# Decoder layer on one core: prologue products and norms, and the order of the attention loop's last output product and first cross scores

## The reference: what is computed

```python
x = x + self_attn(layernorm(x))          # 16 query heads of 32, 4 key/value heads, rope, softmax, @ W_out
x = x + cross_attn(layernorm(x), ctx)    # q = ln(x @ Wq) per head; k = ln(ctx[:345] @ Wk); v = ctx[:345] @ Wv
                                         # plus a second softmax over the last 16 rows ("dca"), added; @ Wo
x = x + moe(layernorm(x))                # shared expert (1408) + top 4 of 60 experts (352), router on x
```

## Time and profile before

| | |
|---|---|
| median of three runs | 1272.35 us |
| profiled execution | 1271.59 us, span 1269.8 us |
| TensorE busy | 1128.7 us (89%) |
| VectorE, ScalarE, GpSimd busy | 512.8, 259.0, 369.1 us |
| one pair of the loop (205.85 to 362.91) | 157.06 us |
| the loop begins, the last pair's last output product ends | 47.9, about 682 us |

### The profile page before, as it was taken

The page is one execution under the profiler, slowest core; times in us unless marked ns, Lnnn a source line. Parts: engine busy times, 40 slices in busy tenths (PEclk is TensorE's granted clock), DMA queues, the critical chain, the costliest instruction groups (busy, mean ns, idle before and its releaser), DMA issues.

```text
span 1269.8 us, 19035 instructions
## 1 busy us (share of the span) xinstructions
PE 1128.7 (89%) x5590; PEld 606.8 (48%) x5590; DVE 512.8 (40%) x1411; ACT 259.0 (20%) x804; POOL 369.1 (29%) x843
## 2 busy tenths in 40 slices
PE   1899888998889988999887999999898898998898
PEld 0354455444554445544454555554444454454454
DVE  7652565426654266542754561121121121211144
ACT  0141232412324133241331300011110111111100
POOL 3274460754607545075200036000000000000073
PEclk9898899988999889998899999999999998998999
DMA  8999001000010000100202478399999999999654
GB/s 312 335 396 366 13 2 43 23 1 12 2 52 14 1 12 2 53 14 1 89 1 70 123 283 293 121 334 391 390 394 387 391 390 385 388 385 380 241 137 116
DMA packets 76583, 233.08 MB, mean 184 GB/s; under 512 B 11362, under 2 KB 13766, under 8 KB 68814
## 3 DMA queue, kind: packets, MB, share of 16 engines
q1 hardware_dynamic: 58830, 197.90, 42.6%
q10 hardware_dynamic: 11520, 20.98, 4.6%
q0 software_dynamic: 6144, 13.13, 3.5%
HBM read 178.75 MB, written 53.22 MB: 183 GB/s over the span
## 4 chain that ended last, share of the span: by engine, by line
PE 72%; DVE 10%; DMA 9%; issue 6%; SPq 2%; ACT 1%; DVEq 1%; ACTq 0%
PE ps L817 15%; PE ps L1095 10%; PE ps L899 9%; DMA arena<-in_w 8%; PE ps L1162 6%; PE ps L1158 5%; PE ps L1256 5%; PE ps L1193 3%; PE ps L1189 3%; PE ps L888 2%; PE ps L956 2%; PE ps L976 2%; DVE arena L1748 1%; PE ps L947 1%; PE ps L1150 1%
## 5 line engine op out<-in xcount | busy, mean ns | idle before, releaser
L817 PE MATMUL ps<-arena 128*100 128x512 f32 (+3 forms) x576 | 223.8, 535 | 12.7 <-DVE arena L1719 5.5
L756 POOL DMA_INDIRECT arena<-ys_d,slot_u x32 | 37.7, 1179 | 425.9 <-issue 423.9
L817 PEld LDWEIGHTS ps<-arena 128*100 128x100 f32 (+1 forms) x576 | 89.1, 176 | 116.2 <-issue 96.1
L1162 PE MATMUL ps<-arena 128*64 128x352 f32 x640 | 111.7, 507 | 30.3 <-issue 16.0
L1095 PE MATMUL ps<-arena 128*128 128x400 f32 x352 | 121.7, 508 | 6.8 <-DMA arena<-xT_d 6.0
L899 PE MATMUL ps<-arena 128*100 128x512 f32 x256 | 120.9, 616 | 0.0
L1962 DVE COPY arena<-ps 128x512 f32<-128x512 f32 x40 | 27.7, 692 | 229.0 <-PE ps L1150 229.0
L1158 PE MATMUL ps<-arena 128*128 128x352 f32 x320 | 98.1, 459 | 0.8 <-issue 0.8
L682 POOL TENSOR_TENSOR arena<-arena 115x512 f32<-115x512 f32 (+1 forms) x29 | 30.1, 1039 | 227.5 <-DVE arena L1675 158.2
L1330 ACT ACTIVATE arena<-ps,arena 100x345 f32<-100x345 f32 x128 | 69.3, 546 | 132.2 <-DVE arena L1748 130.7
L1095 PEld LDWEIGHTS ps<-arena 128*128 128x128 f32 x352 | 67.7, 193 | 59.4 <-issue 8.4
(11 more groups left out here) (218 smaller groups left out, 1521.6 us busy)
## 6 DMA issues: line engine op xcount, KB each, us to landing
arena<-in_w SPq DMA_DIRECT2D x60, 1408.0 KB, 12.2
arena<-in_w SPq DMA_DIRECT2D x60, 512.0 KB, 13.3
xs_d<-zero SPq DMA_DIRECT2D x5, 3328.0 KB, 26.2
arena<-in_w SPq DMA_DIRECT2D x60, 192.0 KB, 13.9
arena<-xs_d ACTq DMA_DIRECT2D x40, 256.0 KB, 7.8
ys_d<-arena ACTq DMA_DIRECT2D x40, 256.0 KB, 7.5
ys_d<-zero SPq DMA_DIRECT2D x2, 3328.0 KB, 24.7
arena<-in_se_up SPq DMA_DIRECT2D x11, 512.0 KB, 6.9
```

The lines of the kernel that those rows point to most:

```text
L817: last = nc.tensor.matmul(ps[0:m, k, 0:cols[1] - cols[0]], lhs(c), w[:, c, cols[0]:cols[1]], start=(c == 0), stop=(c == n_c - 1))
L1162: last = nc.tensor.matmul(ps[half * HALF:(half + 1) * HALF, 3 + gu, 0:I], xsT[1][:, c, half * HALF:(half + 1) * HALF], w13_s[s][1 + half][ ...
```

## The change

- Prologue: the six context products stand ahead of the transposes of the dca keys, in banks (2, 3, 5) and (6, 7, 0). The three key norms are one sequence: three squares into one tile of 3 x 512, one sum over it, one inverse root on 48 columns, three scalings.
- TensorE: the fourth part of the first output product stands ahead of kx(1,2) and vx(1,1), which stand behind the transposes of the second sequence's probabilities. vx(1,2), kx(0,0) and the second xT2 stand inside step 0, with two products of zeros behind them. The query projection of sequence 1 goes from step 0 to step 1, vx(0,0) from step 6 to 5. The zeros of steps 1 and 5 go from (0, 2) and (2, 3) to (0, 0) and (0, 2).
- VectorE: the second layernorm of x is interleaved with the four maxima of step 0.
- GpSimd: both dca_blocks stand ahead of head_norm((1, 2)).

The diff, without the lines of the fill table, the names of tiles and ScalarE's order, which follows TensorE's:

```diff
--- before.py
+++ after.py
...
@@ -109,9 +111,9 @@
 
 
 
-STEP_HOOKS = {0: [("xq", 1)], 1: [("kx", 0, 0)], 2: [("kx", 0, 1)], 3: [("xqT", 1)], 4: [("kx", 0, 2), ("ds", 1)],
-              5: [("dpT", 0), ("rx", 0)], 6: [("vx", 0, 0), ("xo", 0)], 7: [("vx", 0, 1)], 8: [("dpT", 1)]}
-STEP_ZEROS = {1: (0, 2), 2: (0, 2), 3: (2, 3), 4: (0, 2), 5: (2, 3), 6: (0, 2), 7: (0, 2), 8: (2, 0)}
+STEP_HOOKS = {1: [("xq", 1)], 2: [("kx", 0, 1)], 3: [("xqT", 1)], 4: [("kx", 0, 2), ("ds", 1)],
+              5: [("dpT", 0), ("rx", 0), ("vx", 0, 0)], 6: [("xo", 0)], 7: [("vx", 0, 1)], 8: [("dpT", 1)]}
+STEP_ZEROS = {1: (0, 0), 2: (0, 2), 3: (2, 3), 4: (0, 2), 5: (0, 2), 6: (0, 2), 7: (0, 2), 8: (2, 0)}
 
 
 def decoder_kernel(nc, x, ctxT, dcaT, W_attn, W_out, b_out, Wq, bq, Wkv, bkv, Wdca, bdca, norm, Wo, bo,
...
...
@@ -720,11 +725,11 @@
                 first_residual(1)
                 head_norm((1, 1))
                 normalise(1)
+                dca_blocks(0)
+                dca_blocks(1)
                 head_norm((1, 2))
-                dca_blocks(0)
                 add_bias(0)
                 head_norm(("q", 0))
-                dca_blocks(1)
                 add_bias(1)
                 head_norm(("q", 1))
                 if more:
@@ -768,18 +773,20 @@
                     last = nc.tensor.matmul(bank(half), c_dca[:, c, :], w_dca[:, c, half * D:(half + 1) * D],
                                             start=(c == 0), stop=(c == CC - 1))
             last.then_inc(dca_mm, 1)
+            pe.wait_ge(kv_centred, 1)
+            pe.wait_ge(c_loaded[0], 16)
+            for c in range(LN_):
+                for n in range(2):
+                    if FIRST_BANKS[n][c] == 0:
+                        pe.wait_ge(dca_n, 2)
+                    for a in range(CC):
+                        last = nc.tensor.matmul(ps[0:LC, FIRST_BANKS[n][c], :], c_in[0][:, a, c * LC:(c + 1) * LC],
+                                                w_kv[:, a, n * D:(n + 1) * D], start=(a == 0), stop=(a == CC - 1))
+                    last.then_inc(first_full, 1)
             pe.wait_ge(dca_n, 3)
             for c in range(DC):
                 last = nc.tensor.transpose(ps[:, 4, c * P:(c + 1) * P], t0[:, c * P:(c + 1) * P], ident[:])
             last.then_inc(dca_t, 1)
-            pe.wait_ge(kv_centred, 1)
-            pe.wait_ge(c_loaded[0], 16)
-            for c in range(LN_):
-                for n, bank_ in ((0, c), (1, (3, 5, 6)[c])):
-                    for a in range(CC):
-                        last = nc.tensor.matmul(ps[0:LC, bank_, :], c_in[0][:, a, c * LC:(c + 1) * LC], w_kv[:, a, n * D:(n + 1) * D],
-                                                start=(a == 0), stop=(a == CC - 1))
-                    last.then_inc(first_full, 1)
             pe.wait_ge(kd_ready, 1)
             pe.wait_ge(w_loaded["w_attn"], 16)
             pe.wait_ge(first_free, 2 * LN_)
@@ -1027,29 +1034,27 @@
                 attend_out(0, 1)
                 values(0, 3)
                 attend_out(0, 2)
-                context_project("kx", 1, 2)
-                context_project("vx", 1, 1)
                 begin("o", 0)
                 end(attend_out(0, 3), "o", 0)
                 transpose_probs(1)
+                context_project("kx", 1, 2)
+                context_project("vx", 1, 1)
                 values(1, 0)
+                key_transpose(1, 0)
                 values(1, 1)
-                key_transpose(1, 0)
                 attend_out(1, 0)
                 transpose_x("xT2", 2, 0)
                 values(1, 2)
                 query_project(0)
+                attend_out(1, 1)
                 key_transpose(1, 1)
-                attend_out(1, 1)
                 values(1, 3)
                 attend_out(1, 2)
-                context_project("vx", 1, 2)
                 begin("o", 1)
                 end(attend_out(1, 3), "o", 1)
+                transpose_normed(("q", 0), ("xqT", 0), S)
                 key_transpose(1, 2)
-                transpose_normed(("q", 0), ("xqT", 0), S)
                 dca_scores(0)
-                transpose_x("xT2", 2, 1)
 
 
                 hooks = {"kx": lambda j, c: context_project("kx", j, c), "vx": lambda j, c: context_project("vx", j, c),
@@ -1060,6 +1065,11 @@
                         four_scores(t)
                     if t in (0, 6):
                         open_context(t // 6)
+                    if t == 0:
+                        context_project("vx", 1, LN_ - 1)
+                        context_project("kx", 0, 0)
+                        transpose_x("xT2", 2, 1)
+                        keep_busy(0, 2)
                     if t == STEPS - 1:
                         spread_T(1)
                     if t >= 2:
...
...
@@ -1605,13 +1616,25 @@
             for c in range(LN_):
                 key = hn[NORMS.index((0, c)) % 3][0:LC, :]
                 dve.wait_ge(first_full, 2 * c + 1)
-                link(nc.vector.tensor_tensor(key, ps[0:LC, c, :], bkv_bc[0:LC, 0:D], ALU.add))
+                link(nc.vector.tensor_tensor(key, ps[0:LC, FIRST_BANKS[0][c], :], bkv_bc[0:LC, 0:D], ALU.add))
                 dve.wait_ge(first_full, 2 * c + 2)
-                link(nc.vector.tensor_tensor(vx[0][0:LC, c, :], ps[0:LC, (3, 5, 6)[c], :], bkv_bc[0:LC, D:2 * D], ALU.add))
+                link(nc.vector.tensor_tensor(vx[0][0:LC, c, :], ps[0:LC, FIRST_BANKS[1][c], :], bkv_bc[0:LC, D:2 * D], ALU.add))
                 dve.sem_inc(first_free, 2)
+
+            three = LN_ * H
+            squares = first_square[0:LC, :]
+            ss = first_stat[0:LC, 0:three]
             for c in range(LN_):
-                key = hn[NORMS.index((0, c)) % 3][0:LC, :]
-                head_norm(key, key, LC, 1.0).then_inc(hn_ready.sem, 1)
+                link(nc.vector.tensor_tensor(squares[:, c * D:(c + 1) * D], hn[c][0:LC, :], hn[c][0:LC, :], ALU.mult))
+            link(nc.vector.tensor_reduce(ss, head(squares), AX, ALU.add))
+            link(nc.vector.tensor_scalar(ss, ss, HD * 1e-6, None, ALU.add))
+            for _ in inverse_root(ss, [first_stat[0:LC, n * three:(n + 1) * three] for n in (1, 2, 3)]):
+                pass
+            for c in range(LN_):
+                slot = NORMS.index((0, c)) % 3
+                nc.vector.tensor_tensor(head(hn[slot][0:LC, :]), head(hn[slot][0:LC, :]),
+                                        ss[:, slot * H:(slot + 1) * H].rearrange("p (a b) -> p a b", b=1).to_broadcast([LC, H, HD]),
+                                        ALU.mult).then_inc(hn_ready.sem, 1)
                 dve.wait_ge(hn_ready.sem, c + 2)
 
             count_[2] = count_[0]
@@ -1775,31 +1798,41 @@
                 maxima(1)
                 for g in range(G):
                     reciprocal(1, g)
+                residual("o", 0)
+                probs_T(1)
                 context_key(1, 2)
-                context_value(1, 1)
-                residual("o", 0)
                 dve.wait_ge(xn_stored[0], i * 16 + 1)
                 dve.wait_ge(x1_ready, i * 2 + 2)
                 wait_normed((2, 0))
                 after_o = norm_x(0)
                 for _ in range(3):
                     next(after_o)
-                probs_T(1)
+                context_value(1, 1)
                 run(after_o)
                 query(0)
-                context_value(1, 2)
+                dca0, dca1 = dca_softmax(0), dca_softmax(1)
                 residual("o", 1)
                 dve.wait_ge(xn_stored[1], i * 16 + 1)
                 wait_normed((2, 1))
-                run(norm_x(1))
-                dca0, dca1 = dca_softmax(0), dca_softmax(1)
+                after_o = norm_x(1)
+                for _ in range(4):
+                    next(after_o)
                 next(dca0)
+                for r in range(4):
+                    next(after_o)
+                    four_max(0, r)
+                    next(after_o)
+                run(after_o)
+                context_value(1, 2)
+                context_key(0, 0)
+                next(dca0, None)
+                next(dca0, None)
                 ahead = [norm_next(0), norm_next(1)]
                 pieces = itertools.chain(*ahead)
                 def few(n):
                     for _ in range(n):
                         next(pieces, None)
-                for t in range(FOURS + 1):
+                for t in range(1, FOURS + 1):
                     if t == FOURS:
                         sums(1)
                         four_T(t - 1, 0)
@@ -1810,29 +1843,25 @@
                     four_max(t, 1)
                     if t == 6:
                         context_T(0)
-                    few(1 if t else 0)
+                    few(1)
                     four_max(t, 2)
-                    if t:
-                        four_T(t - 1, 0)
+                    four_T(t - 1, 0)
                     four_max(t, 3)
                     if t == 7:
                         residual("xo", 0)
                         run(pieces)
```

(23 more changed lines are left out.)

20 lines of the change are left out of this document (13 added, 7 removed).

## The result

The changed kernel takes 1228.06 us (median of four, 1222.64 to 1232.9) against 1271.4: a ratio of 0.9658, 95% interval 0.9613 to 0.9704. That is 43 us less, where 51 were forecast; 1220 was the point, 1228 lies within the range. The same program, measured again beside later experiments, gave 0.9720 (0.9683 to 0.9758).

What follows compares the result with a forecast made beforehand. TensorE, busy 89% of the span, was taken to bound the kernel through its waits and the clock after them. Four pairs at 12.1 us (48.4) plus prologue 3.0 gave 51.4 off 1271.6: 1220 us, eight in ten from 1210 to 1241.

Steps and rivals of the forecast that it cites:

- First place: Last output part ahead of two context products: the 2.94 us wait and lower clock behind it go, net 5.8 a pair.
- the rival of slipping hand-offs: Hand-offs with under 0.7 us of slack slip, taking 5 to 5.5 us a pair: 1241 us, chance 0.12.
- Second place: Second layernorm and step 0: products moved ahead of the transpose remove idle time and lower clock, net 5.2 us a pair.
- Third: Steps 2 and 3: query transpose newly waits 1.3 to 2.0 us on GpSimd's norm, other waits go; 0.5 a pair charged.
- rival (a): The new step 3 wait cools TensorE's clock, costing 2.5 us a pair: 1230 us, chance 0.22.
- Fourth: Steps 5 and 6: three zero products and a 0.8 wait go, a 0.8 bank wait comes; net 1.2 us a pair.
- rival (e): In the loop the clock never falls and hand-offs meet: 13.5 us a pair, 1212 us, chance 0.09.
- Prologue: Ahead of the loop: scores of pair 0 come 6.2 us earlier, but a late context load leaves 3.0, between 0 and 6.
- The stage behind: Expert stage after the loop: its weight loads start relative to its products, so the whole gain passes through.

Runs made afterwards that it cites:

- first_place: The kernel before with one move alone: kx(1,2) and vx(1,1) behind the transposes of the second probabilities, the last output part ahead of them; 0.9795 of before.
- no_interleave: The changed kernel with VectorE's second layernorm run to its end ahead of the dca maxima and the maxima of step 0; 0.9697 of before.
- after_again: The changed kernel itself, unedited, measured again in a later session; 1228.67 us, 0.9720 of before.
- zeros_first: The changed kernel with zero products ahead of the waits of steps 3, 4, 5 and 7 and fewer behind them; 1214.48 us, 0.9566 of before.
- loop_only: The changed kernel with the prologue of before; 0.9691 of before.
- context_early: The changed kernel with the load of the second pair's first context started before the prologue's zero fills instead of behind them; 0.9696 of before.
- zeros_early: The edits of zeros_first and context_early together on the changed kernel; 1215.35 us, 0.9581 of before.
- warm: zeros_early with 18 zero products ahead of TensorE's idle time before the loop and 16 ahead of that before the shared expert; 1228.94 us, 0.9712 of before.
- warm_sized: zeros_first with 9 zero products ahead of TensorE's idle time before the loop and 8 before the shared expert's products; 1215.49 us, 0.9597 of before.

## Why the prediction was right, and where it was not

The forecast, faster with some 4% by the loop, came out; its 51.4 us were 43.

**First place, right, low by 1.2.** "Net 5.8" became 7.0 in first_place. The hand-overs met, and the rival of slipping hand-offs (1241) fell: no layernorm wait, clock 1.00. Up to step 0 the pair is 6.0 us ahead in first_place; the other 0.9 comes in step 0, where the clock was up sooner (xq(1) took 3.90 us, before 4.77).

**Second place, right.** With the first it was to save 11.0 by step 1, and 0.9 of work was to leave that stretch for step 1; the pair is 13.0 ahead there. Taking the first place's 7.0 and the 0.9 from that leaves 5.1 for the 5.2 predicted. no_interleave shows that the interleaving of VectorE's steps did not do it; that leaves the moved products, which no run takes alone. The wait for the second layernorm, charged at 0.9 with ScalarE's copy, is 0.4 (that copy).

**Third, the failing step.** "A new wait of 1.3 to 2.0 us ... I charge 0.5": the wait came, 1.44 us, worked out rightly from GpSimd's 9.4 us. What went wrong is the sentence "Single waits of 1.08 and 1.7 us are not followed by a lower clock", taken as if that made such waits safe in the new order. It was read from one pair, and it isn't so in all pairs of the kernel before. In its last pair the same wait for the sums was followed by the lower clock, with a granted clock of 0.72 from 646 to 652 us:

```profile
645.45 0.56 PE L987 MATMUL ps<-ident,arena 100*128 100x100 f32 x4 [1.66 <-ACT arena L1293]
645.85 1.29 PE L976 MATMUL ps<-zero 128*128 128x200 f32 x4
...
647.68 2.13 PE L976 MATMUL ps<-zero 128*128 128x200 f32 x6
```

Steps 1 to 3 took 20.0 us in the changed kernel and 18.3 in after_again against 17.4 before. With the 0.9 of work that moved into step 1, the 0.4 wait that went from it and the 0.5 charged, 1.0 more was predicted: after_again, with the clock up, has just that (0.9), and the changed kernel 1.5 more than that, the price of the clock. This was rival (a), whose 1230 is nearer to 1228 than the forecast.

**Fourth, the same cause.** "Net 1.2" became 0.2 lost over steps 4 to 6 (25.9 us against 25.7), though three zero products went. The bank wait of vx(0,0), "0.8 added", was 0.59. But behind the sums' wait, 1.67 before and 1.80 now, the clock fell, which costs 1.3 us on vx(0,0)'s four records alone; and so it did, in this pair, behind the old wait of 1.37 in step 7. In zeros_first, with the clock up, steps 4 to 6 take 24.5 us, the 1.2 that was forecast, and a pair 143.05 to 143.44 us, 13.6 to 14.0 under before, where rival (e), "the clock never falls", had 13.5. That kernel has other counts of zero products, so that the numbers meet so closely is partly luck. (e) was near in its price and wrong that the kernel as changed would have it.

**Prologue, right in its parts, high in the sum.** The loop starts at 42.08 ("near 42 us"); the idle time before it is 6.72 (6.7); the price of the low clock behind it 2.06 on the products and 0.7 on the transposes, against 2.6 in all; the scores of pair 0 come 8.3 us earlier, not 6.2. The wait of 3.09 us for the last key block had the lower clock behind it (twelve records 4.19 us, now 2.55), which the sum left out, and the trace of before was 1.3 us late there: loop_only and first_place, with the same prologue, reach these scores at 67.07 and 67.25, not 68.33. "Waits 2.6 us" is 3.42 on the context, landing near 126, and the low clock behind it took 3.38 for four records, 1.5 more. Of "I take 3.0, between 0 (cold and late) and 6" at most 1.5 arrived, its lower end: that much is left at pair 1's scores, and loop_only ends its loop with the changed kernel. context_early shows the cap itself, since pair 0 falls to 147.5.

**The stage behind.** "The whole gain passes through" held for the loop (the rest 591 against 587) within what that stage varies by itself. With a still earlier loop, in context_early and zeros_early (the rest 596 and 603), it did not show; that part of the prediction is open beyond the change as it stood.

**The sum.** A pair was to save 12.1 and saved 10.3 (loop_only): 1.1 more than predicted ahead of step 1 (the first place's 1.2), 1.5 less in steps 1 to 3, 1.4 less in steps 4 to 6. Four such pairs lack 7.2 us. The loop's end came 42.5 us earlier for the 51.4 predicted; the other 1.7 is put down to the prologue (3.0 became 1.3), as what four pairs of 10.3 leave of the 42.5. The medians, 7.9 above 1220.2, agree with these 8.9 within what the stage behind varies by. That it missed by no more is in part luck: what the first place gave beyond its price made up for more than a third of the 2.9 us a pair that steps 1 to 6 fell short by.

## What to carry to other kernels

When a move takes work from one wait and creates a shorter one elsewhere, price what TensorE does in the few us behind the new wait at both clocks, even if single waits of that size left the clock up in the pair that was read of the trace of before, and look at all pairs of it. Where such waits can't be removed, zero products that end just inside them are cheap and can be worth as much as a reordering (11 us of the loop here); size them from a row of the same form, since a filling that overruns costs at least what it overruns (some 10.5 us past two waits, and 13.6 us of time, in warm). A gain ahead of a load that is queued late is no gain until the load is moved, and here moving it shortened the loop by 7 us but not the time.

## What the runs showed of the hardware

- What TensorE's clock does behind a wait does not follow from the wait's length. The same wait (1.44, 1.44 and 1.45 us) was followed by the lower clock in one execution's pair 1 and not in its pair 3 nor in pair 1 of another execution: four zero records took 1.54 us in the one case and 0.87 in the others. The wait for the sums (1.66 and 1.67 us) was followed by it in one of four pairs of the kernel before, and (1.66 to 1.98 us) in all eight pairs of the changed kernel's two executions; the bank's 1.37 us in none of four before and in four of those eight. One pair, and one trace, do not tell whether a wait of this size is harmless.
- With 17 or 34 products more around the loop, TensorE sat up to 1.9 us at the loop's first instruction with no wait shown; in no other kernel here did it sit more than 0.2 us so. The instruction queue on the profile's page fits with it: 42 packets in all others, 43 in warm_sized, 46 in warm.

```profile
q8 instruction: 46, 0.75, 0.3%
```

That the loop's instructions were fetched again is argued from these counts, not shown.
- A VectorE product of one column, with both inputs in SBUF, beside a GpSimd product of 512 took 0.98 us against 0.15, as in the trace of before (0.90). The Trainium skill, SBUF — State Buffer, "Who interferes with whom", says that a VectorE instruction with two SBUF inputs and a GpSimd instruction that reads SBUF contend, and that the port pair they share is locked by one of them at a time; the trace agrees again.
